# Cross-scan layers: where the third injection, its decay and the softplus products are made

## What is computed

```python
xin, z = split(x @ in_proj)               # 192 inner channels; pixels read row by row and column by column,
xs = 4 sequences of L = 1024              # each forwards and backwards
dts, Bs, Cs = x_proj(xs)                  # ranks 12, 16, 16
delta = softplus(dt_proj(dts) + bias)
h = exp(delta * A) * h + delta * Bs * u   # for each of 192 channels and 16 states, along L
y = sum over states of h * Cs + u * Ds
y = layer norm(sum of the 4 directions) * silu(z) @ out_proj
```

## Time and profile before

| what | us |
|---|---|
| median of 3 runs (3808.05 to 3823.39) | 3813.99 |
| the profiled execution | 3815.76 |
| its span, first to last instruction | 3813.9 |
| VectorE (DVE) busy | 3266.3 |
| GpSimd (POOL) busy | 2350.1 |
| ScalarE (ACT) busy | 2051.3 |
| TensorE (PE) matmuls busy | 2849.4 |

### The profile page before, as it was taken

One profiled execution on the slowest core, in us unless ns is written; L12 is line 12 of the kernel. 1 busy time (PEld: TensorE's weight loads), 2 busy tenths in 40 slices (PEclk: granted clock), 3 DMA queues, 4 the chain that ended last, 5 costly groups with the idle time before them and its releaser, 6 DMA issues. The chain is left out here.

```text
span 3813.9 us, 26717 instructions
## 1 busy us (share of the span) xinstructions
PE 2849.4 (75%) x6084; PEld 648.1 (17%) x6084; DVE 3266.3 (86%) x2104; ACT 2051.3 (54%) x2278; POOL 2350.1 (62%) x1004
## 2 busy tenths in 40 slices
PE   6778777877887788435667677688778887887887
PEld 2111111111111211111111121111111111111111
DVE  1899999999999998585988924999999999999993
ACT  3465555656565655314555425556565556656562
POOL 1677767777776776003656504677676767776773
PEclk9677787878788877767789777677887778788778
DMA  2555546463655554103443405365546555564742
GB/s 57 136 126 139 138 125 143 119 161 97 160 129 133 124 133 117 28 0 84 117 106 85 99 5 122 99 160 133 129 115 142 135 128 126 132 153 109 157 119 62
DMA packets 140377, 436.95 MB, mean 115 GB/s; under 512 B 33429, under 2 KB 34139, under 8 KB 139915
## 3 DMA queue, kind: packets, MB, share of 16 engines
q1 hardware_dynamic: 140234, 435.53, 47.4%
HBM read 307.50 MB, written 6.82 MB: 82 GB/s over the span
## 5 line engine op out<-in xcount | busy, mean ns | idle before, releaser
L841 POOL TENSOR_TENSOR L_read<-L_state,L_c_rows 128x1024 f32<-128x1024 f32 x768 | 1809.0, 2362 | 757.1 <-DVE L_state L931 467.3
L931 DVE TENSOR_TENSOR_SCAN L_state<-L_decay,L_b_ps 128x1024 f32<-128x1024 f32 x768 | 1756.0, 2286 | 29.4 <-DVE L_b_ps L916 2.1
L651 PE MATMUL L_y_ps<-L_read,L_fold 128*64 128x512 f32 x3072 | 1255.0, 913 | 394.8 <-POOL L_read L841 375.5
L916 DVE TENSOR_TENSOR L_b_ps<-L_du,L_b_ps 128x1024 f32<-128x1024 f32 x768 | 937.5, 1221 | 236.0 <-issue 146.4
L777 ACT ACTIVATE L_decay<-L_delta,L_a_neg 128x1024 f32<-128x1024 f32 x768 | 876.4, 1145 | 406.7 <-DVE L_state L931 405.7
L767 ACT COPY L_b_ps<-L_b_rows 128x1024 f32<-128x1024 f32 x256 | 260.1, 1016 | 340.6 <-DVE L_state L931 220.6
L651 PEld LDWEIGHTS L_y_ps<-L_read,L_fold 128*64 128x64 f32 x3072 | 188.0, 161 | 1356.5 <-POOL L_read L841 1017.6
L1461 POOL TENSOR_TENSOR L_read<-L_state,L_c_rows 128x1024 f32<-128x1024 f32 x96 | 237.3, 2477 | 184.3 <-PE L_y_ps L1257 109.5
L1567 DVE TENSOR_TENSOR_SCAN L_state<-L_decay,L_b_ps 128x1024 f32<-128x1024 f32 x96 | 219.5, 2286 | 3.3
L626 PE MATMUL L_side_ps<-L_dbl,L_w_dt 128*128 128x512 f32 x216 | 182.4, 940 | 50.3 <-DVE L_sq_b L902 26.9
L626 PE MATMUL L_side_ps<-g_cm,L_w_u 96*128 (+1 forms) x216 | 179.7, 921 | 41.7 <-ACT L_u L695 40.0
(11 more groups left out here) (315 smaller groups left out, 2677.3 us busy)
## 6 DMA issues: line engine op xcount, KB each, us to landing
L_c_rows<-L_bc_dram SPq DMA_DIRECT2D x580, 256.0 KB, 4.0
L_b_rows<-L_bc_dram SPq DMA_DIRECT2D x580, 256.0 KB, 4.2
L_delta<-L_delta SPq DMA_DIRECT2D x204, 256.0 KB, 5.8
L_du<-L_du SPq DMA_DIRECT2D x140, 256.0 KB, 5.8
L_du<-L_u SPq DMA_DIRECT2D x64, 256.0 KB, 6.1
L_bc_dram<-L_dbl SPq DMA_DIRECT2D x40, 128.0 KB, 3.4
L_delta<-L_delta_a SPq DMA_DIRECT2D x16, 256.0 KB, 4.4
L_du<-L_du_a SPq DMA_DIRECT2D x16, 256.0 KB, 5.5
```

The costliest lines, as they stand in the source:

```text
L651: m = nc.tensor.matmul(y_ps[i * BLK:(i + 1) * BLK, c, :], fold[:, :], y_half(t, o, i), start=first, stop=last, skip_group_check=True)
L841: nc.gpsimd.tensor_tensor(read[:, t % READS, :], state[:, t % STATES, :], c_rows[:, g % 2, :], ALU.mult).then_inc(multiplied, 1)
L916: nc.vector.tensor_tensor(to[:, :], du2[:, d * NBLK + c, :], row[:, :], ALU.mult).then_inc(injected, 1)
L931: nc.vector.tensor_tensor_scan(state[:, t % STATES, way], decay[:, t % DECAYS, way], fed[:, way], 0.0, ALU.mult, ALU.add).then_inc(scanned, 1)
```

## The change

Both cross layers are changed; the rest of the network is not. GpSimd makes the injection of c = 2 (`inject_c`), from du2 and b_rows in SBUF into the state buffer, ahead of its read of c = 0 of the same group; the scan of c = 2 then runs in place there. Its decay goes to PSUM (`work_ps`), which it shares with the injection of c = 0, and ScalarE waits for that scan. The row of B has one PSUM copy (`row_ps`), in which the injection of c = 1 is made in place; b_rows has two buffers in SBUF. GpSimd no longer forms du within the turns: VectorE multiplies each half of a sum in `side_ps` by u three tiles after its slot, and ScalarE copies the half to delta five tiles after it (in place of four; at most at tile 47), and waits for the product. SyncE's block copies wait for that copy (`delta_ready`).

```diff
-POOL_SOFTPLUS = [{29: ("gap", 0), 36: ("gap", 1), 37: ("du", 0), 39: ("gap", 2), 41: ("du", 1), 45: ("du", 2)},
-                 {22: ("gap", 0), 28: ("gap", 1), 32: ("du", 0), 34: ("gap", 2), 35: ("du", 1), 39: ("du", 2)}]
+POOL_GAP = [{29: 0, 36: 1, 39: 2}, {22: 0, 28: 1, 34: 2}]
...
-        decay = sb("decay", [128, DECAYS, L])
+        decay = sb("decay", [128, DECAYS - 1, L])
-        b_rows = sb("b_rows", [128, L])
+        b_rows = sb("b_rows", [128, 2, L])
-        b_ps = [ctx.enter_context(nc.psum_tensor(f"{name}_b_ps{i}", [128, L], F32)) for i in range(2)]
+        row_ps = ctx.enter_context(nc.psum_tensor(f"{name}_row_ps", [128, L], F32))
+        work_ps = ctx.enter_context(nc.psum_tensor(f"{name}_work_ps", [128, L], F32))
...
-        MULT0, SCAN0, SUM0, INJECT0 = NBLK + 1, DECAYS, READS, 1
+        MULT0, SCAN0, SUM0, INJECT0, READY0 = NBLK + 1, DECAYS, READS, 1, 2
...
@@ -506,7 +507,10 @@
             def copy_block(n, q):
                 j, half = q // 2, q % 2
                 rows = slice(half * BLK, half * BLK + BLK)
-                sp.wait_ge(sp_du, n * NJ + j + 1)
+                if isinstance(n, int) and n == 0:
+                    sp.wait_ge(sp_du, j + 1)
+                else:
+                    sp.wait_ge(delta_ready, n * NJ + j + 1)
                 for side in range(2):
                     to = slice(side * BLK, side * BLK + BLK)
...
@@ -523,10 +527,11 @@

                 d, p = g // NP, g % NP
                 sp.wait_ge(b_ready, G + 1)
+                sp.wait_ge(injected_c, G + 1)
                 for h in range(2):
                     row = p + NP * h
-                    sp.dma_start(b_rows[h * BLK:(h + 1) * BLK, :],
-                                 bc_dram[order, d, row:row + 1, :].to_broadcast([BLK, L])).then_inc(b_in, 16)
+                    sp.dma_start(b_rows[h * BLK:(h + 1) * BLK, g % 2, :],
+                                 bc_dram[order, d, row:row + 1, :].to_broadcast([BLK, L])).then_inc(b_in[g % 2], 16)

...
                 elif kind == "sum":
+                    if not isinstance(turn, Head):
+                        act.wait_ge(sp_du, 2 * (turn.next * NJ + j) + i + 1 - NJ)
                     ins = nc.scalar.copy(delta[:, j, s], side_ps[:, :])
+                    if i == 1:
+                        ins.then_inc(delta_ready, 1)
+                        act.wait_ge(delta_ready, turn.next * NJ + j + 1)
+                        act.sem_inc(side_free, 1)
+                        return
                 elif kind == "z":
...

-            def copy_b(G, g):
-
-                act.wait_ge(b_in, 32 * (G + 1))
+            def copy_b(number, G, g):
+
+                act.wait_ge(b_in[g % 2], (number * (GROUPS // 2) + g // 2 + 1) * 32)
                 act.wait_ge(scanned, (G - 1) * NBLK + 2 + SCAN0)
-                nc.scalar.copy(b_ps[g % 2][:, :], b_rows[:, :]).then_inc(b_ready, 1)
+                nc.scalar.copy(row_ps[:, :], b_rows[:, g % 2, :]).then_inc(b_ready, 1)

                 for t, (d, p, c) in enumerate(tiles):
                     if c == 1:
-                        copy_b(number * GROUPS + p + NP * d, (p + NP * d))
+                        copy_b(number, number * GROUPS + p + NP * d, p + NP * d)
                     if p == 0:
                         act.wait_ge(delta2_in[d * NBLK + c], (number + 1) * PER_BLOCK)
                     act.wait_ge(scanned, number * NT + t - DECAYS + 1 + SCAN0)
-                    nc.scalar.activation(decay[:, t % DECAYS, :], delta2[:, d * NBLK + c, :], ACT.Exp,
+                    g = t // NBLK
+                    if c == 2:
+
+                        act.wait_ge(scanned, number * NT + t - 1 + SCAN0)
+                    to = work_ps if c == 2 else decay[:, c, :]
+                    nc.scalar.activation(to[:, :], delta2[:, d * NBLK + c, :], ACT.Exp,
                                          scale=a_neg[:, o * 2 + d, c, p:p + 1]).then_inc(decay_ready, 1)
                     for at, key, i in turn.sides:
-                        if at == t - ACT_LAG and key[0] in ACT_SIDES:
+                        if t == min(at + ACT_LAG + (key[0] == "sum"), NT - 1) and key[0] in ACT_SIDES:
                             take(turn, key, i)
...
-            def softplus(turn, kind, j):
+            def gap(turn, j):
                 n = turn.next * NJ + j
-                if kind == "gap":
-                    pool.wait_ge(sp_log, n + 1)
-                    pool.wait_ge(sp_less, n + 1)
-                    l = l_of[j]
-                    nc.gpsimd.tensor_tensor(l[:, :], more[:, :], l[:, :], ALU.subtract).then_inc(sp_gap, 1)
-                else:
-                    wait_side(pool, turn.use(("sum", j), 1))
-                    if not isinstance(turn, Head):
-                        for q in range(2 * j, 2 * j + 2):
-                            pool.wait_ge(du2_in[q], turn.next * PER_BLOCK)
-                    nc.gpsimd.tensor_tensor(du[j], delta[:, j, :], u[:, j, :], ALU.mult).then_inc(sp_du, 1)
+                pool.wait_ge(sp_log, n + 1)
+                pool.wait_ge(sp_less, n + 1)
+                l = l_of[j]
+                nc.gpsimd.tensor_tensor(l[:, :], more[:, :], l[:, :], ALU.subtract).then_inc(sp_gap, 1)
...
+            def inject_c(number, g):
+
+                d, last = g // NP, NBLK - 1
+                if g % NP == 0:
+                    pool.wait_ge(du2_in[d * NBLK + last], (number + 1) * PER_BLOCK)
+                pool.wait_ge(b_in[g % 2], (number * (GROUPS // 2) + g // 2 + 1) * 32)
+                pool.wait_ge(multiplied, (number * GROUPS + g) * NBLK + MULT0)
+                nc.gpsimd.tensor_tensor(state[:, last, :], du2[:, d * NBLK + last, :], b_rows[:, g % 2, :],
+                                        ALU.mult).then_inc(injected_c, 1)

             def turn_of(turn):
                 number = turn.number
                 for t in range(NT):
                     g = t // NBLK
+                    if t % NBLK == 0:
+                        inject_c(number, g)
                     pool.wait_ge(scanned, number * NT + t + 1 + SCAN0)
                     if t % NBLK == 0:
                         pool.wait_ge(c_in[g % 2], (number * (GROUPS // 2) + g // 2 + 1) * 32)
-                    if t in POOL_SOFTPLUS[turn.r]:
-                        softplus(turn, *POOL_SOFTPLUS[turn.r][t])
-
-            for kind, j in (("gap", 0), ("gap", 1), ("du", 0), ("gap", 2), ("du", 1), ("du", 2)):
-                softplus(Head(), kind, j)
+                    if t in POOL_GAP[turn.r]:
+                        gap(turn, POOL_GAP[turn.r][t])
+
+            def form_du(j):
+
+                wait_side(pool, Head().use(("sum", j), 1))
+                nc.gpsimd.tensor_tensor(du[j], delta[:, j, :], u[:, j, :], ALU.mult).then_inc(sp_du, 1)
+
+            gap(Head(), 0)
+            gap(Head(), 1)
+            form_du(0)
+            gap(Head(), 2)
+            form_du(1)
+            form_du(2)
             over_turns(pool, turn_of)
             add_x(Tail())
...
+                if kind == "sum" and i == 0:
+                    for q in range(2 * j, 2 * j + 2):
+                        dve.wait_ge(du2_in[q], turn.next * PER_BLOCK)
                 dve.wait_ge(side_ready, use + 1)
+                if kind == "sum":
+                    nc.vector.tensor_tensor(du[j][:, s], side_ps[:, :], u[:, j, s], ALU.mult).then_inc(sp_du, 1)
+                    return
...
-                row = b_ps[g % 2]
                 if p == 0:
                     dve.wait_ge(du2_in[d * NBLK + c], (number + 1) * PER_BLOCK)
                 if c == 0:
-                    dve.wait_ge(b_ready, number * GROUPS + g + 2)
-                to = row if c == 2 else b_ps[1 - g % 2]
-                if c < 2:
+                    dve.wait_ge(b_ready, number * GROUPS + g + 1 + READY0)
+                to = row_ps if c == 1 else work_ps
+                if c == 0:
                     dve.wait_ge(scanned, T + SCAN0)
-                nc.vector.tensor_tensor(to[:, :], du2[:, d * NBLK + c, :], row[:, :], ALU.mult).then_inc(injected, 1)
+                nc.vector.tensor_tensor(to[:, :], du2[:, d * NBLK + c, :], row_ps[:, :], ALU.mult).then_inc(injected, 1)
+                dve.wait_ge(injected, (number * GROUPS + g) * 2 + c + 1 + INJECT0)
...
-                    T = number * NT + t
+                    T, g = number * NT + t, t // NBLK
                     for at, key, i in turn.sides:
-                        if at == t - DVE_LAG and key[0] in ("cent", "shift", "out"):
+                        if at == t - DVE_LAG and key[0] in ("sum", "cent", "shift", "out"):
                             finish_side(turn, key, i)
-                    fed = inject_tile(number, t)
-                    dve.wait_ge(injected, T + 1 + INJECT0)
+                    if c < 2:
+                        by, fed = decay[:, c, :], inject_tile(number, t)
+                    else:
+                        by, fed = work_ps, state[:, c, :]
```

(12 more changed lines are left out.)

12 lines of the change are left out of this document (6 added, 6 removed).

## The result

The changed kernel takes 3911.12 us (median; 3910.55 to 3912.61) beside 3814.72 us for the kernel before: a ratio of 1.026 (95% interval 1.0244 to 1.0276), so it is slower by 2.6%, and not faster by 1.4% as forecast.

A forecast was written before the change was run, and what follows sets the result against it. GpSimd was to replace VectorE as the bound; its operations, injection waits and sum waits gave turns of 175.6 and 171.2 us, 53 us less over eight of each: 3763, or 3761 as median; range 3650 to 3850.

The forecast's parts named there:

- rival 3: Slower, by the single side bank: each of six sums costs 7.7 us of wait, 89 us more, 3903; chance 0.14.
- Costs of the operations: VectorE's group takes 9.33 us, a half product 669 ns, the scan stays 2286 ns; GpSimd issues every 2.33 us.
- the injections' own waits: GpSimd's injection waits for its own read before it, taken as 0.1 us each, 1.6 us per turn.
- GpSimd becomes the bound: With its injections' waits, GpSimd needs 160.3 us per row-order and 158.0 per column-order turn, against 180.5 and 172.9 now.
- The waits at the sums: Late second halves of softplus sums hold GpSimd's reads: 13.3 us per row-order turn, 13.2 per column-order turn.
- the ring: Where ScalarE's slot falls on c2: scan ends, decay 1.15 us, copy 0.58, second half on TensorE, fold, read.
- I add 2 for the first sum and for the pieces of tiles 12 to 27: In the row-order turn, 2 us of further waits on GpSimd, bringing the turn's waits to 15.3 us.
- The clock: TensorE's second halves after a stop run near 1.2 GHz, those following work at 2.4: 5.2 against 2.8 us.
- The 70 us set on this: With TensorE at the high clock level throughout, 70 us less over 16 turns, giving 3691.
- The late row copy: The 4.6 us wait for a row copy, late by the row's DMA, goes, as load_b goes out one group earlier.

The follow-up runs named there:

- e2: The changed kernel with the third injection left out, GpSimd only signalling and scan c2 fed with the copied delta*u block: 3857.6 us, ratio 1.011.
- e1: The changed kernel with work_ps for decay c2 alone, VectorE's injections in place in row_ps, that of c1 adding: 3723.1 us, ratio to the kernel before 0.976.
- e6: e3 with work_ps left to decay c2 alone, by the same edit as e1: 3786.3 us, ratio 0.993.
- e9: e5 with side pieces whose slot plus four falls on c2 copied a tile earlier, sums and gate products left out: 3734.6 us, ratio 0.980.
- e10: e5 with two row-order slots moved, the first half of dt 0 from 22 to 21 and one GpSimd gap from 36 to 37: 3734.5 us, ratio 0.980.
- e5: The changed kernel with sums copied four tiles after their slot in place of five, products staying on VectorE: 3775.8 us, ratio 0.991.
- e3: The changed kernel with products back on GpSimd and sums copied four tiles after their slot, so only the injection moves: 3800.2 us, ratio 0.997.

## Why the prediction was wrong

The forecast was 3761 us and the result is 3911; it lies near the 3903 of rival 3, which had a chance of 0.14. That nearness is luck: rival 3 had the six sums of an image cost 46.2 us of waits, and they cost 24.9.

- **Costs of the operations**: right. The group is 9.3 us, an injection on GpSimd 2.36, a product 0.69, the scan unchanged. GpSimd's operations of two turns come to 315.1 us (158.7+156.4), its waits to 50.3; of the 368.7 us of the two turns 3.3 are left, beside the 3.2 taken for the injections' own waits (2 x 1.6).
- **"GpSimd becomes the bound"**: wrong for row order. e2 took 37 us of its work out of each turn, and row-order turns stayed at 189. What holds up the folds sets them, and GpSimd's waits are its shadow. In column order the load matters.
- **The waits at the sums**: right, and at the places named. Forecast 13.3 and 13.2 us, measured 10.9 and 14.0. Singly: 3.7, 0.6, 7.7 and 0.6 forecast for reads 42, 43, 45 and 46, measured 2.4, 0.7, 6.6 and 0.7; 5.4 and 6.5 forecast for reads 34 and 39, measured 5.3 and 6.8. The rows of the ring at read 45:

```profile
1369.57 1.12 ACT L794 ACTIVATE L_work_ps<-L_delta,L_a_neg 128x1024 f32<-128x1024 f32 x1 [4.21 <-DVE L_state L971]
...
1370.62 0.58 ACT L713 COPY L_delta<-L_side_ps 128x512 f32<-128x512 f32 x1
1371.25 2.08 PE L631 MATMUL L_side_ps<-L_gate_a,ident 128*128 128x512 f32 x2 [6.57 <-ACT L_delta L713]
...
1375.87 0.69 DVE L929 TENSOR_TENSOR L_u<-L_side_ps,L_u 128x512 f32<-128x512 f32 x1 [6.34 <-PE L_side_ps L631]
...
1376.59 0.58 ACT L713 COPY L_delta<-L_side_ps 128x512 f32<-128x512 f32 x1 [5.40 <-DVE L_u L929]
1377.02 2.36 POOL L863 TENSOR_TENSOR L_read<-L_state,L_c_rows 128x1024 f32<-128x1024 f32 x1 [6.63 <-PE L_y_ps L656]
```

Decay 47 has waited 4.21 us for scan 45, the copy of the first half ends at 1371.2, TensorE had stopped for 6.57 us and makes the second half by 1375.76 (4.5 us, for which I took 5.2), VectorE had stood for 6.34 us before its product, and GpSimd 6.63 us before read 45.

- **"I add 2 for the first sum and for the pieces of tiles 12 to 27"**: this step failed. All other waits together cost a row-order turn 19.8 us and a column-order turn 5.6, for which the sum had 2 and 0. That is 21.8 us an image with the sums' small errors (50.3 measured, 28.5 forecast), 174 us over eight images; the two first turns, which have no finish and took 172.8 and 172.5 us, give some 30 back. The rows gave a warning: read-outs already waited 289 us for folds, 36 an image. The waits have two sources. The first is the ring that I had found (a slot plus lag that falls on c2, followed soon by another piece) and used for the sums alone. It holds as well for dt 0 followed by the variance, 6.4 us at reads 25 and 26: the wait at read 25 goes with work_ps free (e1, e6), with that piece taken a tile earlier (e9) and with its slot moved (e10). The second is TensorE's own work, for which the sum had no term: reads 4 and 5, 6.9 us at the low level of the clock against 1.4 at the high one, and most of the column-order turn's 5.6, which did not shrink in e1 and e9. The 2.9 us at tiles 14 to 20 and the rest at tiles 0 to 2 I did not take apart.
- **The clock**: as forecast, the pieces behind stops ran at the low level (2.07 and 2.08 us for two matmuls at 1286.24 and 1371.25, against 1.13 in the earlier trace rows). The 70 us set on this were not tried by themselves, and they left out the z pieces: in the row-order turn before, the granted clock was 0.80 over the first 25 us (1160.8 to 1185.8), in the changed kernel 0.50. The Trainium skill, "TensorE: Matmul & The Clock Gate", section "HAM oscillation — how this bites in real kernels", says that a TensorE which stops for a wait in each round of a loop starts each round slow; the rows behind the stops of 3.25 and 6.57 us agree.
- **The late row copy** of the earlier trace rows did go: ScalarE waited 118 us for rows before, 14 in the changed kernel. VectorE's waits for the copies did not shrink (69 us, 89 after), and it was not where the time was decided.

The cause, as the runs show it: two changes close one ring. Decay c2, which waits for scan c0, moves ScalarE back within its queue, and the sums' copies, a tile later, move onto just these tiles. Take away either, the shared tile (e1, -188 us) or the late copy (e5, -135 us), and the kernel beats the one before. Some of e1's gain, 2.8 us a turn at read 5, came by the clock. Beside the ring stands TensorE's own work on the z, u and bc pieces, which GpSimd now feels. That reads 4 and 5 follow the clock is shown by turns of one run (e3); why the changed kernel has it low there in all six row-order turns with a finish stays open, and no run held it fixed.
